# A sampling loop on one Trainium2 core: factors spread by row groups, three banks for selections, GpSimd's sums in a row, the softplus sum behind a tile's third product

## The reference

```python
x = x + L0(gn(x))   # attention over super-tokens
x = x + L1(gn(x))   # grouped 3x3 convolution with routed expert weights
x = x + L2(gn(x))   # deformable sampling, then a selective scan
x = x + L3(gn(x))   # 3x3 convolution and 1x1 on the masked channels
```

```python
xc     = silu(dwconv(in_proj(x)))                      # 3x3 depthwise
offset = gelu(layer_norm(dwconv(xc))) @ off_w.T + off_b  # a (dx, dy) per pixel and group of channels
xd     = bilinear_sample(xc, pixel + offset)           # four taps
xs     = xd.reshape(B, C, L)
dts, Bs, Cs = split(x_proj_w @ xs, [8, 9])             # 8 rows, 1 row, 1 row
delta  = softplus(dt_w @ dts + dt_bias)                # C x L
h[l]   = exp(delta[l] * A) * h[l-1] + delta[l] * Bs[l] * xs[l]
y[l]   = Cs[l] * h[l] + Ds * xs[l]
out    = out_proj_w @ layer_norm(y)
```

## Time and profile before

| | |
|---|---|
| median of the runs | 2436.45 us (2435.26 to 2442.39) |
| the profiled execution | 2439.82 us, its span 2438.0 us |
| mean granted clock of TensorE | 0.929 of full speed |
| busy over the span | PE 2135.2 us (88%), DVE 1834.2 (75%), ACT 1416.5 (58%), POOL 1417.2 (58%) |
| L948, POOL's sums in the loop | 320 of 1272 ns |
| L856, DVE's products in the loop | 576 of 682 ns |
| L1074, PE's sums in the loop | 512 instructions (two for one fp32 matmul) |

### The profile page before, as it was taken

The page is one execution under the profiler, slowest core; times in us unless marked ns, Lnnn a source line. Parts: engine busy times, 40 slices in busy tenths (PEclk is TensorE's granted clock), DMA queues, the critical chain, the costliest instruction groups (busy, mean ns, idle before and its releaser), DMA issues. The chain is left out here.

```text
span 2438.0 us, 28756 instructions
## 1 busy us (share of the span) xinstructions
PE 2135.2 (88%) x7363; PEld 1102.2 (45%) x7363; DVE 1834.2 (75%) x3128; ACT 1416.5 (58%) x2192; POOL 1417.2 (58%) x1305
## 2 busy tenths in 40 slices
PE   2998759798998999997988978698989799999798
PEld 2397435443553444433335954353435434444243
DVE  6555667499986999995755658566999589999754
ACT  1843444286884777763346437235868667777532
POOL 2233009398967989972322410484989499999532
PEclk9978879899998999998998979799989799999899
DMA  5000283500001212224820006534000022223244
GB/s 189 1 1 0 92 302 94 199 1 1 1 1 28 44 39 61 40 52 141 251 45 0 1 1 233 189 107 158 0 1 1 12 27 53 48 44 61 83 122 113
DMA packets 199339, 172.78 MB, mean 71 GB/s; under 512 B 72535, under 2 KB 175327, under 8 KB 195831
## 3 DMA queue, kind: packets, MB, share of 16 engines
q1 hardware_dynamic: 199159, 170.78, 24.8%
HBM read 81.69 MB, written 72.29 MB: 63 GB/s over the span
## 5 line engine op out<-in xcount | busy, mean ns | idle before, releaser
L948 POOL TENSOR_TENSOR BIG<-BIG 128x512 f32<-128x512 f32 x320 | 407.1, 1272 | 88.4 <-DVE BIG L856 78.4
L856 DVE TENSOR_TENSOR BIG<-PSUM,BIG 128x512 f32<-128x512 f32 x576 | 391.0, 682 | 59.0 <-PE PSUM L1066 30.7
L1138 DVE SCALAR_TENSOR_TENSOR PSUM<-BIG,VECS,PSUM 128x1024 f32<-128x1024 f32 x224 | 288.2, 1287 | 44.6 <-PE PSUM L2111 39.5
L1074 PE MATMUL PSUM<-BIG,CSTS 128*128 128x512 f32 x512 | 266.8, 602 | 0.0
L782 POOL TENSOR_TENSOR BIG<-TOEP,BIG 128x384 f32<-128x384 f32 x84 | 98.2, 1196 | 270.5 <-DVEq L1543 270.5
L2111 PE MATMUL PSUM<-BIG,WDW 128*128 128x512 f32 x512 | 236.4, 607 | 11.1 <-ACT BIG L2011 11.1
L1066 PE MATMUL PSUM<-BIG,SELB 120*128 120x512 bf16 x576 | 212.0, 386 | 16.7 <-issue 6.8
L2307 PE MATMUL PSUM<-BIG 128*128 128x381 f32 (+1 forms) x576 | 189.5, 493 | 12.9 <-DVE BIG L789 12.9
L1066 PEld LDWEIGHTS PSUM<-BIG,SELB 120*128 120x128 bf16 x576 | 55.3, 96 | 264.4 <-DVE BIG L856 190.9
L2111 PEld LDWEIGHTS PSUM<-BIG,WDW 128*128 128x128 f32 x512 | 99.3, 195 | 141.1 <-issue 122.4
L1784 POOL TENSOR_TENSOR BIG<-BIG 128x1024 f32<-128x1024 f32 x64 | 151.1, 2360 | 10.3 <-POOL BIG L1787 10.3
(11 more groups left out here) (363 smaller groups left out, 5079.6 us busy)
## 6 DMA issues: line engine op xcount, KB each, us to landing
spill<-X SPq DMA_DIRECT2D x18, 1024.0 KB, 6.1
back_spill<-BIG SPq DMA_DIRECT2D x32, 576.0 KB, 3.4
X<-x SPq DMA_DIRECT2D x32, 512.0 KB, 7.5
rows_spill<-X SPq DMA_DIRECT2D x64, 256.0 KB, 4.1
out<-BIG SPq DMA_DIRECT2D x64, 256.0 KB, 3.6
BIG<-rows_spill SPq DMA_DIRECT2D x28, 512.0 KB, 5.3
X<-back_spill SPq DMA_DIRECT2D x14, 896.0 KB, 12.8
BIG<-fc SPq DMA_DIRECT2D x8, 1024.0 KB, 10.0
```

Of the source, the lines that this page charges most:

```text
L856: dve.tensor_tensor(img(product_buffer(b, q)), img(PSUM[:, (k + q) % 2, :]), pch(c, XBASE, dy, dx), ALU.mult).then_inc(df_p, 1)
L948: pool.tensor_tensor(a, a, x, ALU.add).then_inc(df_add, 1)
L1074: pe.matmul(PSUM[:, ACC, :], ident, product_buffer(b, m), start=(m == 0), stop=(m == PE_SUMS - 1)).then_inc(df_acc, 1)
L1138: return dve.scalar_tensor_tensor(out=rows8(to), in0=strip(c, base, dy, dx), scalar=vc(weights, j), in1=rows8(acc), op0=ALU.mult, op1=ALU.add)
```

## The change

- **Factors by row groups.** WZ, WB and WC go. One matmul WX (128 columns of weights, of which 3 x 32 are used) gives the ten rows of x_proj three times, in rows 0 to 31, 32 to 63 and 64 to 95 of bank ZB. ACT copies these 96 rows to SBUF. Then three matmuls of 32 rows each, one from each group of rows, make z, Bs and Cs in three banks, with the weights in WG: dt_w in the first group, ones in the other two. WG is loaded by six small transfers behind the loads of x; the load of dt_w at the front and the small matmul that multiplied it with x_proj go.
- **Three banks for the selections.** Bank 7, until now the projection's own, becomes a third bank for `spread`; spread q waits for product q - 3. The projection writes the bank MB of the layer norm.
- **GpSimd's sums in a row.** POOL does the weights' splits of tile T + 2 first, then four of its sums one behind the other, then UU, then the fifth sum.
- **The softplus sum** of DVE moves from the end of the step to behind product 2 of the next step; the dBx product and the scan follow products 3 and 4.
- PE's order changes with it: the mean goes behind the second sum, the projection from ahead of WZ to behind WX. ACT's order changes too.

The core of the diff:

```diff
+        SPREADS = (0, 1, 7)
...
+            for s in range(2):
+                at, cols = s * XR, slice(s * C, (s + 1) * C)
+                sp.dma_start(WG[at:at + DT_RANK, cols], dts[:, 2 * C:3 * C]).then_inc(load, 16)
+                for r in (1, 2):
+                    row = r * 32 + at + DT_RANK + r - 1
+                    sp.dma_start(WG[row:row + 1, cols], cst[0:1, CST["one"][0]:CST["one"][0] + C]).then_inc(load, 16)
             sp.dma_start(rt_spill, RT).then_inc(rt_saved, 16)
...
                 product(2)
                 if on(-2):
+                    dve.wait_ge(sc_ln, after(T - 2))
+                    dve.wait_ge(sc_u, after(T - 3))
+                    dve.wait_ge(sc_da, after(T - 3))
+                    dve.tensor_tensor(RL, PSUM[:, ZB, :], AB, ALU.add).then_inc(sc_delta, 1)
+                product(3)
+                if not far:
+                    product(4)
+                if on(-2):
                     dve.wait_ge(sc_u, after(T - 2))
-                    dve.wait_ge(sc_bc, after(T - 2))
+                    dve.wait_ge(sc_zbc, all_three(T - 2))
                     dve.tensor_tensor(PSUM[:, BB, :], UU, PSUM[:, BB, :], ALU.mult).then_inc(sc_bx, 1)
-                product(3)
-                if on(-2):
...
-                        pe.wait_ge(df_p, turn(T, q - 2))
-                        pe.matmul(img(PSUM[:, (k + q) % 2, :]), SELB[:, q, :], WTB[0:WROWS, k, :, h, :],
+                        if q >= 3 or on(-1):
+                            pe.wait_ge(df_p, turn(T, q - 3))
+                        pe.matmul(img(PSUM[:, SPREADS[q % 3], :]), SELB[:, q, :], WTB[0:WROWS, k, :, h, :],
...
-                    pe.matmul(PSUM[:, ZB, :], WZ[:, :], XS[:, (k + 1) % 2, :], start=True, stop=True).then_inc(sc_z, 1)
-                spread(6)
+                    pe.matmul(PSUM[:, ZB, :], WX[:, :], XS[:, (k + 1) % 2, :], start=True, stop=True).then_inc(sc_xd, 1)
+                spread(7)
+                if on(-3):
+                    pe.wait_ge(sc_lv, after(T - 3))
+                    pe.matmul(PSUM[:, MB, :], WOUT2[:, :], YY, start=True, stop=True).then_inc(sc_proj, 1)
                 if not far:
                     add_up(3)
-                spread(7)
-                if on(-1):
-                    pe.matmul(PSUM[:, BB, :], WB[:, :], XS[:, (k + 1) % 2, :], start=True, stop=True)
                 spread(8)
                 if on(-1):
+                    pe.wait_ge(sc_copied, copied(T - 1, 0))
                     pe.wait_ge(sc_y, after(T - 2))
-                    pe.matmul(PSUM[:, CB, :], WC[:, :], XS[:, (k + 1) % 2, :], start=True, stop=True).then_inc(sc_bc, 1)
+                    settle(pe)
+                    for r, bank in enumerate((ZB, BB, CB)):
+                        rows = slice(r * 32, r * 32 + 32)
+                        pe.matmul(PSUM[:, bank, :], WG[rows, :], AB[rows, :], start=True, stop=True).then_inc(sc_zbc, 1)
```

More of the change, by code:

```diff
@@ L866, in step @@
                     dve.wait_ge(sc_t, after(T - 4))
[L867 removed]
+                    dve.scalar_tensor_tensor(out=xch(c - 4), in0=img(PSUM[:, MB, :]), scalar=OUTB[:, :], in1=xch(c - 4),
                                              op0=ALU.add, op1=ALU.add,
@@ L882, in step @@
                                            ALU.mult, ALU.add).then_inc(sc_h, 1)
[L883 to L889, removed]
+                if far:
+                    if on(-1):
+                        if on(0):
+                            dve.wait_ge(df_acc, summed(T, PE_SUMS - 1, PE_SUMS))
+                        dve.wait_ge(df_add, summed(T - 1, POOL_SUMS - 1, POOL_SUMS))
+                        far_dve(dve, c - 1, (k + 1) % 2, reach)
+                    product(4)
                 if on(-2):
@@ L995, in step @@
                     act.preload_act_table_set("natural_log_exp_and_others")
-                if on(-3):
-                    act.wait_ge(sc_cen, after(T - 3))
-                    act.wait_ge(sc_t, after(T - 4))
-                    act.activation(RS2, PSUM[:, MB, :], ACT.Square).then_inc(sc_sq, 1)
+                if on(1):
+                    act.wait_ge(df_r1, after(T + 1))
+                    act.activation(part(1), top(REST), ACT.Copy).then_inc(df_mid, 1)
                 if on(2):
@@ L1078, in step @@
                 spread(1)
-                if on(-3):
-                    pe.wait_ge(sc_y, after(T - 3))
-                    pe.wait_ge(sc_lv, after(T - 4))
-                    pe.matmul(PSUM[:, MB, :], cs("center"), YY, start=True, stop=True).then_inc(sc_cen, 1)
                 spread(2)
@@ L1086, in step @@
                 add_up(1)
+                if on(-3):
+                    pe.wait_ge(sc_y, after(T - 3))
+                    pe.wait_ge(sc_x, after(T - 4))
+                    pe.matmul(PSUM[:, MB, :], cs("center"), YY, start=True, stop=True).then_inc(sc_cen, 1)
                 spread(4)
+                add_up(2)
+                spread(5)
                 if on(-3):
@@ L1090, in step @@
                     pe.matmul(PSUM[:, MB, :], cs("mean"), RS2, start=True, stop=True).then_inc(sc_var, 1)
-                    pe.wait_ge(sc_x, after(T - 4))
-                    pe.matmul(PSUM[:, OB2, :], WOUT2[:, :], YY, start=True, stop=True).then_inc(sc_proj, 1)
-                add_up(2)
-                spread(5)
+                spread(6)
                 if far:
@@ L1173, in _ @@
             dve.reg_mov(far_dve_turn, 0)
-            dve.wait_ge(load, 16 * 9)
-            for w in (WQ, WK, WV, WPROJ, WIN, WOUT, WZ, WB, WC):
+            dve.wait_ge(load, 16 * 8)
+            for w in (WQ, WK, WV, WPROJ, WIN, WOUT, WX, WG):
                 dve.memset(w[:, :], 0.0)
@@ L1250, in _ @@
             dve.wait_ge(const_pe, 1)
-            for s in range(2):
-                p, q = s * C, s * C + C
-                dve.tensor_copy(WZ[p:q, p:q], PSUM[p:q, 0, 0:C])
             dve.tensor_copy(OUTB[:, :], PSUM[:, 1, 0:1])
@@ L2076, in _ @@
             credit(pe, sp_lgt, sp_tr, sp_fold, o_tr, o_mm, cv_mm)
-            credit(pe, df_w, df_acc, sc_z, sc_bc, sc_cen, sc_proj, sc_var)
+            credit(pe, df_w, df_acc, sc_xd, sc_zbc, sc_cen, sc_proj, sc_var)
             pe.reg_mov(far_pe_turn, 0)
             pe.reg_mov(far_pe_done, 0)
-            pe.wait_ge(load, 16 * 9)
+            pe.wait_ge(load, 16 * 8)
             pe.wait_ge(const_dve, 9)
-            pe.matmul(PSUM[:, 0, 0:C], DTS[:, 0:2 * C], DTS[:, 2 * C:3 * C], start=True, stop=True)
             pe.matmul(PSUM[:, 1, 0:1], PLAIN[:, :], vc("out_ln_b"), start=True, stop=True)
@@ L2391, in _ @@
                 keep_busy(BUSY[2], 5)
+                pe.wait_ge(load, 16 * 14)
                 pe.wait_ge(rad_dve, pair * 16 + 16)
```

108 lines of the change are left out of this document (53 added, 55 removed).

## The result

The changed kernel takes 2525.07 us (median of 4 runs, 2520.58 to 2528.54), the kernel before, with a fourth run beside it, 2439.15 (2435.26 to 2442.39): ratio 1.0352, 95% interval 1.0326 to 1.0378. The change makes it slower by 86 us; the prediction was 2514, range 2475 to 2560. The profiled execution took 2520.58 us (span 2518.7), against 2518 for the sum made on the profiled execution of before.

The account below looks back on a forecast made before the run. PE was taken as full, DVE nearly (10.87 us a tile); a new loop of waits would make 12.0. Tiles 72 + pass ends 4 + start 2 = 78 us: 2518 for the profiled execution, 2514 as median, range 2475 to 2560.

Parts of the forecast that it names:

- The loop: Sampling loop: sum, UU, dBx, scan, WX, selection, projection, YY and rest of step close a chain of 11.95 us a tile.
- The second loop: Chain through PE alone behind the scan: 11.64 us a tile plus the row-group seams, 11.94 with seams of 0.3.
- the 0.42 of the prediction: In the loop through PE: time from selection 0 to its product on DVE, 0.42 us.
- Row groups: PE's three 32-row matmuls run side by side in 0.86 us; PE's own work 10.0 instead of 10.6 us a tile.
- s = 0.3: Both seams into and out of the row-group mode on PE, 0.3 us a tile at full clock; ends 0 and 1.0.
- the rival in program order: Row groups start in order: three matmuls take 1.72 us, 12.8 a tile, 2566 us; chance 0.10.
- s = 0.54: Price if PE drains wholly at both row-group seams: 0.54 us, giving 12.18 us a tile.
- The dBx product: On DVE: two products give 1.8 us where POOL's answer takes 2.07, so dBx waits 0.27 us.
- the 0.5 us of dBx, scan and Cs in a row: DVE's extra waits from the late softplus sum, which alone would fit: 10.28 + 0.53 = 10.81 us a tile.
- ends of the passes: Last tile's softplus has copy and group ahead of it: 2 us a pass, 4 in all; ends 0 and 8.
- three banks: Selections wait for product q-3: removes PE's 0.3 us of short waits, a gain only where PE is the bound.
- The start: Front of the kernel: six more small transfers ahead of the spills, partly given back: 2 us later, ends 0 and 4.

Follow-up runs that it names:

- experiment 2: Changed kernel with PE running the output projection ahead of WX, which still waits for the scan: 2489.42 us, ratio to the kernel before 1.0220.
- Experiment 1: Changed kernel with WX no longer waiting for the scan of the tile before: 2462.72 us, ratio to the kernel before 1.0113.
- experiment 3: Changed kernel with full factors WZ, WB and WC, no 96-row copy and no row groups: 2549.67 us, ratio to the kernel before 1.0463.
- experiment 5: Kernel before with the late softplus sum, ACT's exponential in the next step and UU behind four sums: 2500.84 us, ratio 1.0271.
- experiment 7: Changed kernel with the softplus sum back at the end of DVE's step, behind product 8: 2831.03 us, ratio to the kernel before 1.1629.
- experiment 8: Changed kernel, WX free of the scan, four engines reordered, Cs product to SBUF so the group need not wait for YY: 2437.24 us, ratio 1.0017.

## Why the prediction was right

**The loop.** Each term of 11.95 has its reading in the rows above. Sum to scan 0.76 + 1.31 + 0.74 = 2.81, as predicted. Scan to WX 1.42 (1.35 predicted), WX 0.94 (0.97), selection 0.22, projection to YY 1.12 (1.08), YY 0.67 (0.65), the rest of the step 4.86 (4.87). Sum 12.04. No term is off by more than 0.07.

**The second loop.** Selection 0 starts at 889.98; with the 0.42 of the prediction its product could start at 890.40, and it starts at 888.68 + 3 x 0.60 = 890.48, behind the products ahead of it. So the loop over YY decides by less than 0.1 us, and the two loops are as close as the prediction had them (11.95 and 11.94). Cutting the first loop alone can therefore gain next to nothing: experiment 2 gained 0.51 us a tile because it shortened the second one too, until the wait for ACT's Ln held it at 11.56. Experiment 1 took the scan out of both and reached 11.18.

**Row groups.** The sum came out: selection 888.60 + 0.22 = 888.82, next selection 889.98, so 1.16 for a group that was put at 0.86 with seams of 0.3. Its parts did not: only 0.09 of the 0.3 lies ahead of the group and none behind it, and the group itself takes 1.07 instead of 0.86, so that s = 0.3 was right in part by luck. The three do run side by side; the rival in program order, with 1.72 and more, is out. Matmul by matmul the starts do come in order here (888.914, 888.920, 888.927); only, the first halves of the second and third lie ahead of the second half of the first (889.447). The Trainium skill ("TensorEngine Tiling (Array Packing)", Key Properties) says that changing the tiling mode drains TensorE. The seams of s = 0.54, the prediction's price for a whole drain at both, are not seen: 0.09 ahead of the group is all that stands at a seam.

**The dBx product** starts 0.27 later than the pace allows (881.50 + 3 x 0.60 = 883.30, and it starts at 883.57), as predicted; the 0.19 in brackets is the part of that in which DVE stood idle. Whether the 0.5 us of dBx, scan and Cs in a row would be harmless by themselves, as the prediction had it, no run shows alone: experiment 1 keeps them and takes 11.18 us a tile, with POOL's fifth sum as its bound.

**Where the sum was off.** From the start of the first selection of a pass to the start of its last residual sum the first pass took 412.7 us instead of 366.5 and the second 408.0 instead of 366.5: together 87.7, where the prediction had 76. From the first to the last softplus sum it is 78.2 (72 predicted; the first tile of pass one took 14.3). The rest, 9.5, is the term "ends of the passes", put at 4 with 8 as its upper end: 3.3 at the fronts, 6.2 at the drains. Its working had only the softplus's longer way through copy and group, and *three banks* counted only what the third bank gives and not what it takes, the projection's own bank. The drain of the first pass, PE in the kernel before (L1082 center, L1090 mean, L1092 projection) and in the changed one (L1104, L1110, L1126):

```profile
1103.81 1.12 PE L1082 MATMUL PSUM<-BIG,CSTS 128*128 128x512 f32 x2 [0.91 <-DVE BIG L897]
1105.63 1.71 PE L1090 MATMUL PSUM<-BIG,CSTS 128*128 128x512 f32 x2 [0.69 <-ACT BIG L999]
1107.13 1.91 PE L1092 MATMUL PSUM<-BIG,WOUT 128*128 128x512 f32 x2
```

```profile
1141.07 2.05 PE L1104 MATMUL PSUM<-BIG,CSTS 128*128 128x512 f32 x2 [3.62 <-DVE X L876]
1143.81 2.07 PE L1110 MATMUL PSUM<-BIG,CSTS 128*128 128x512 f32 x2 [0.69 <-ACT BIG L1022]
1146.66 2.08 PE L1126 MATMUL PSUM<-BIG,WOUT 128*128 128x512 f32 x2 [0.78 <-ACT BIG L1031]
```

Before, the center follows YY, and the projection the mean at once. Now the center waits for the residual sum of the tile before (it writes the bank that this reads), and the projection for ACT's Ln; and all three run at 1.2 GHz (granted clock 0.50 from 1138.5 on). From the last softplus sum to the last residual sum 12.65 us became 15.65. Start to start, the center comes 1.50 us later behind YY, the mean 0.92 later behind the slower center, and the projection 1.35 later behind the mean, while YY comes 0.93 earlier; so the clock has a share in the loss beside the bank. The drain is 15.1 to 16.2 in all five variants of the changed kernel with a late sum, without the row groups too (experiment 3: 15.1 and 15.4), and 12.6 and 13.0 in experiment 5, where the projection has its own bank. In the full loop of the changed kernel these waits are covered; at the drain nothing covers them. This is read from the traces; giving the projection its bank back was not tried.

**The start** was put at +2, and the first selection comes 6.5 us earlier (736.8 instead of 743.3). But in the profiles of the other eight kernels it lies between 736.1 and 742.4, with the changed front and with the old one, so no term of the change can be told here. It does explain why the profiled execution, at 2520.58, came so close to 2518: the passes took 11.7 us more than predicted and the start, in this profile, 8.5 less. That is luck. By the medians the change costs 86 us where 78 were forecast.

## What to carry to other kernels

When a change takes work from a full engine, follow the chain of waits once around through the new order, and add it up: here 0.6 us less of PE work a tile was bought with a scan that came 1.0 us too late for the matmul behind it. Ask of each wait what it protects: WX had inherited WZ's wait for the scan, although only the factors behind it write what the scan reads, and that one line held 62 of the 86 us. A bank that two stages share, so that a third gets one, can cost nothing in the steady loop and still be paid where the loop runs empty; in experiment 2 it was paid in the loop itself, as soon as the order changed.

## What the runs showed of the hardware

- The three 32-row fp32 matmuls of 512 columns start within 0.013 us of each other (888.914 to 888.927), and so do their second halves, 0.533 later. A half of a matmul of 128 rows takes 0.43 (0.86 for both); one of 32 rows was not run alone. So of the 0.30 of extra cost 0.09 lies ahead of the group and 0.11 in each half, none behind it.
- Behind a wait of 3.12 us in each tile TensorE's clock was at 1.2 GHz for a part of every tile (experiment 7, mean granted clock 0.80), and an expected loss of some 140 us against the changed kernel became 306.
- DVE's YY takes 0.85 us (median of 13) instead of 0.75 with its second operand in SBUF (experiment 8, where the order around it is new too), while the product with Cs, now written to SBUF, takes 0.69 instead of 0.70.
